# Attention 0: the softmax probabilities, split into fp16 halves, are transposed by DMA instead of by TensorE

## The chip, the cores and the metric

The kernel runs on one core of one Trainium2 chip. The metric is the device time of one execution in microseconds (us); lower is better. A core has TensorE (PE in the profile, with its weight loads as PEld), VectorE (DVE), ScalarE (ACT), GpSimd (POOL) and SyncE (SP), and 16 DMA engines that all queues share. An engine works through its own instructions in the order of the program and waits on semaphores.

## What is computed

A two-layer decoder over 32 sequences of 64 tokens of width 512. The change touches only the first attention, which has 32 query heads and 8 key/value heads of width 128:

```python
def _L0_xattn_ref(query, value, wq, wk, wv, wo):
    q = (query @ wq).reshape(b, tq, HQ, D)
    k = (key @ wk).reshape(b, tk, HKV, D)      # key = value = ctx_4096
    v = (value @ wv).reshape(b, tk, HKV, D)
    ...
    scores = jnp.einsum('bqhd,bkhd->bhqk', q, k)
    probs = jax.nn.softmax(scores, axis=-1)
    out = jnp.einsum('bhqk,bkhd->bqhd', probs, v).reshape(b, tq, HQ * D)
    return out @ wo

x = x + _L0_xattn_ref(_layernorm(x, axis=-1), ctx_4096, L0_xattn_wq, ...)
x = x + _L0_ffn_ref(_layernorm(x, axis=-1), L0_ffn_W0, ...)
x = x + _L1_xattn_ref(_layernorm(x, axis=-1), ctx_4096, ctx_4096, ...)
x = x + _L1_ffn_ref(_layernorm(x, axis=-1), L1_ffn_weight, ...)
```

Matrix products with fp32 accuracy are made from fp16 halves: a value is kept as high and low fp16 part, and a product takes three passes, high with high, high with low, low with high (`PASSES`).

## The kernel before

`attention0` walks over 8 groups (one key/value head and its 4 query heads) and in each over 4 blocks of 512 tokens (`t`, 8 sequences of 64). One block of one group is called a stage here; there are 32. Groups 0 to 6 run in a hardware loop (`Fori`), group 7 is written out. The stage is software-pipelined by hand: while the softmax of stage t runs on DVE and ACT, PE projects the queries, keys and values of the next stage. The order on PE in a stage, which no scheduler changes, is:

- `scores` (L534, into `sc`), for two pairs of heads, `jp` 0 and 1;
- `project` of the next stage, units 0 to 3: one query head each (L520, into the two banks `pj`; unit u waits until the low half of unit u-2 has left the same bank);
- `transpose_probs` (L543): eight 128x128 fp32 transposes of the probabilities `E` into the banks `tv`;
- in two stages of a group `transpose_weights` (L583), which prepares weights of the FFN that follows;
- `project` unit 4 (the keys, L520), `weigh_values` for the first half (L561, into `tv`), `project` unit 5 (the values, L525), `weigh_values` for the second half, and `project_out` (L572, into `xp`), which has 48 matmuls of 512 columns.

On DVE and ACT the scores lose their maximum (L743, L745), pass through the exponential (ACT, L666), and are summed, inverted and scaled (L751, L753, L755: `normalise`, which raises `p_done`). `E` holds [128 query rows of two heads, jp, 8 sequences, 64 keys] in fp32. After the transposes ACT copies `tv` to the high half of `PT` (L681) and DVE takes the low half (L788); `weigh_values` waits for `tp_lo`. Every projected unit leaves `pj` the same way: high half by ACT (L649, L651, L653), low half by DVE (L709, L712). `OT` is the weighted sum (L658, L718), `X` the residual that DVE adds to (L805). Once a group, at t = 0, the output weights are split: ACT L674, DVE L780.

SyncE's queue issues all DMAs: the weights of the next group (`load_qkv`, `load_o`), the FFN weights (L474, L476), and the stores of the prepared FFN weights (L481, L483).

Of the kernel before, what the change touches and what calls it, by code (L numbers as in the profile page):

```python
# [15 lines left out]
F16 = mybir.dt.float16  # L16
# [3 lines left out]
ALU = mybir.AluOpType  # L20
ACT = mybir.ActivationFunctionType
# [402 lines left out]
def attention0(nc, sb, pb, sem, X, ident, XT, CT, w0, w1, w0t_dram, w1t_dram, ahead_of_ffn0,  # L424
# [5 lines left out]
    with ExitStack() as ph:  # L430
# [7 lines left out]
        V = sb(ph, "V", [P, 2, 2, BT, HEAD0], F16)  # L438
        E = sb(ph, "E", [P, 2, BB, SEQ], F32)
        ST = sb(ph, "ST", [P, 3, 2, BB], F32)  # L440
        PT = sb(ph, "PT", [P, 2, BT, REP * SEQ], F16)
        OT = sb(ph, "OT", [P, 2, REP, BLOCK], F16)

        words = bits16(XB)
# [9 lines left out]
        names = ("o_hi o_lo sc_done pj_done tp_done pv_done xp_done "  # L454
                 "exp_done pj_hi tp_hi ot_hi max_done sub_done sum_done rcp_done p_done pj_lo tp_lo ot_lo x_acc "
                 "wb_ld wb2_ld wa_done wstep ww_done wcut wbits wm_done wsum wqs_done wq_done wt_done wt_hi wt_lo w_st")
        S = {n: sem(ph, "a0_" + n) for n in names.split()} | weight_sems
        block = ph.enter_context(nc.Block())
# [4 lines left out]
        def prepared(t, last):  # L463

            return [] if last else [(n, lo, hi) for n, (at, lo, hi) in enumerate(PREP) if at == t]

        def n_of(g, t, per, c):

            return g * (SPG * per) + (t * per + c)

        @block.sync
        def _(sp):
            with sp.Fori(0, GROUPS - 1) as g:
                sp.dma_start(WB[:, 0:8, :].rearrange("p (t c) k -> p t (c k)", t=2),  # L474
                             w0[bass.ds(g * 256, 256), :].rearrange("(t p) k -> p t k", p=P)).then_inc(S["wb_ld"], 16)
                sp.dma_start(WB[:, 8:16, :].rearrange("p (t c) k -> p t (c k)", t=4),  # L476
                             w1[:, bass.ds(g * 256, 256)].rearrange("(t p) k -> p t k", p=P)).then_inc(S["wb2_ld"], 16)
                sp.wait_ge(S["qkv_lo"], g * 2 + 2)
                load_qkv(sp, g + 1)
                sp.wait_ge(S["wt_lo"], g * 4 + 4)  # L480
                sp.dma_start(w0t_dram.rearrange("p (s c n) -> p s c n", s=2, c=KC)[:, :, :, bass.ds(g * 256, 256)],  # L481
                             WS0[:, :, :, :]).then_inc(S["w_st"], 16)
                sp.dma_start(w1t_dram.rearrange("p (s c n) -> p s c n", s=2, c=IC)[:, :, bass.ds(g * 2, 2), :],  # L483
                             WS1[:, :, :, :]).then_inc(S["w_st"], 16)

                sp.wait_ge(S["w_st"], g * 32 + 32)
                sp.wait_ge(S["o_lo"], g + 1)
                load_o(sp, g + 1)

            sp.wait_ge(S["qkv_lo"], 2 * GROUPS)  # L490
            sp.wait_ge(S["o_lo"], GROUPS)
            sp.dma_start(W0T[:, :, :, :], w0t_dram.rearrange("p (s c n) -> p s c n", s=2, c=KC)).then_inc(w0_ld, 16)

        @block.gpsimd
        def _(pool):
# [10 lines left out]
        def _(pe):  # L506
# [28 lines left out]
                                             KT[:, ka, b, :], start=n == 0, stop=n == 2)  # L535
                    last.then_inc(S["sc_done"], 1)

            def transpose_probs(g, t):
                pe.wait_ge(S["p_done"], n_of(g, t, 2, 2))
                for i in range(BT):  # L540
                    for jp in range(2):
                        at = (i % 2) * 256 + jp * P
                        last = pe.transpose(tv[i // 2][:, at:at + P],  # L543
                                            E[:, jp, 2 * i:2 * i + 2, :], ident[:, :])
                    if i % 2:
                        last.then_inc(S["tp_done"], 1)

            def weigh_values(g, t, pair):

                if pair == 0:
                    pe.wait_ge(S["pj_lo"], n_of(g, t, 6, 6))
                    pe.wait_ge(S["tp_lo"], n_of(g, t, 2, 2))
                else:
                    pe.wait_ge(S["ot_lo"], n_of(g, t, 4, 2))
                for s in range(2):
                    for n, (a, b) in enumerate(PASSES):
                        for h in range(2):
                            rows = slice(h * SEQ, (h + 1) * SEQ)  # L560
# [25 lines left out]
            def group(g, last):  # L586
                for t in range(SPG):
                    nxt = (g, t + 1) if t < SPG - 1 else (g + 1, 0)
                    more = not (last and t == SPG - 1)
                    scores(g, t)  # L590
                    if more:
                        project(*nxt, range(4))
                    transpose_probs(g, t)
# [39 lines left out]
        def _(act):  # L633
# [26 lines left out]
            def group(g, last):  # L660
                for t in range(SPG):
                    nxt = (g, t + 1) if t < SPG - 1 else (g + 1, 0)
                    more = not (last and t == SPG - 1)
                    for jp in range(2):
                        act.wait_ge(S["sub_done"], n_of(g, t, 2, jp + 1))
                        act.activation(E[:, jp, :, :], E[:, jp, :, :], ACT.Exp, scale=exp_scale).then_inc(S["exp_done"], 1)  # L666
                        if more:
                            high(*nxt, (jp,))
                    for p in prepared(t, last):
                        weights_times_rec(g, *p)  # L670
                    if t == 0:
# [3 lines left out]
                    if more:  # L675
                        high(*nxt, range(2, 4))
# [15 lines left out]
                    high_out(g, t, 1)  # L692
                    if t == SPG - 2 and not last:
                        high_kv(act, g + 1)
                    if last and t == SPG - 1:
                        first_x[0](act)

            high(0, 0, range(6))
            with act.Fori(0, GROUPS - 1) as g:
                group(g, False)  # L700
# [3 lines left out]
        def _(dve):  # L704
# [43 lines left out]
            def normalise(g, t, jp):  # L748
# [6 lines left out]
                dve.tensor_tensor(E[:, jp, :, :], E[:, jp, :, :], ST[:, 2, jp, :].unsqueeze(2).to_broadcast([P, BB, SEQ]),  # L755
                                  ALU.mult).then_inc(S["p_done"], 1)

            def group(g, last):
                for t in range(SPG):
                    nxt = (g, t + 1) if t < SPG - 1 else (g + 1, 0)  # L760
# [6 lines left out]

                    scores_less_max(g, t, 0)
                    scores_less_max(g, t, 1)
                    if more:  # L770
                        low(*nxt, 0)
                    normalise(g, t, 0)
                    if more:
                        low(*nxt, 1)
                    normalise(g, t, 1)
                    if more:
                        low(*nxt, 2)
                    if t == 0:
# [3 lines left out]
                    x_ahead(0)  # L782
                    if more:
                        low(*nxt, 3)
                    x_ahead(1)
# [1101 lines left out]
```

## Time and profile before

| | before |
|---|---|
| median of 3 runs | 1853.54 us (1852.3 to 3521.8) |
| profiled execution | 1853.57 us |
| its span | 1851.8 us |
| PE busy / DVE busy / ACT busy | 90% / 71% / 42% of the span |
| attention 0 (first to last of its stages) | about 60 to 1069 us of the span |

The span is the time from the first to the last instruction of the profile; the execution's time has 1.8 us around it. A row of a timeline has the start, the time that the engine was busy with this group of instructions, the engine, the line of the kernel and the operation as output<-input; a bracket at its end says how long the engine sat idle before it and what released it.

### The profile page before, as it was taken

How to read it: one execution, taken by the hardware profiler on the slowest of the kernel's cores; microseconds unless marked ns; L12 is line 12 of the kernel's file. 1: busy time of each engine (PE TensorE's matmuls, PEld its weight loads, DVE VectorE, ACT ScalarE, POOL GpSimd, SP SyncE). 2: the span in 40 equal slices, each digit the busy share in tenths (PEclk: the TensorE clock that was granted, in tenths of full speed). 3: DMA queues.
4: the chain of work that ended last, by engine and by line, in shares of the span. 5: the costliest groups of instructions: out<-in, count | busy, mean ns of one | idle time of the engine just before them, and what ended most of it. 6: DMA issues, size and time to landing. Idle time of an engine off the chain costs nothing. (4 is left out here: it accounts for less than half of the span.)

```text
span 1851.8 us, 31064 instructions
## 1 busy us (share of the span) xinstructions
PE 1666.5 (90%) x11590; PEld 936.3 (51%) x11590; DVE 1312.0 (71%) x2451; ACT 780.0 (42%) x1692; POOL 326.0 (18%) x266
## 2 busy tenths in 40 slices
PE   4899999999999999999999778999998696888793
PEld 4455555555555555555555434555554354555451
DVE  6567666776675666656757669887887535999688
ACT  3324242333243333423332245666665323555451
POOL 2001000010010000000100011111110224777414
PEclk8899999999999999999999889999999898999897
DMA  6100202002002020020030020000002001000002
GB/s 238 46 1 22 71 1 92 1 1 92 1 1 92 1 80 13 1 92 1 1 126 1 1 80 1 1 1 0 0 0 58 0 1 35 1 0 0 0 1 91
DMA packets 41663, 57.69 MB, mean 31 GB/s; under 512 B 1618, under 2 KB 23379, under 8 KB 41300
## 3 DMA queue, kind: packets, MB, share of 16 engines
q1 hardware_dynamic: 41556, 56.11, 8.9%
q8 instruction: 86, 1.41, 0.3%
q14 instruction: 21, 0.17, 0.0%
HBM read 44.57 MB, written 11.53 MB: 30 GB/s over the span
## 5 line engine op out<-in xcount | busy, mean ns | idle before, releaser
L520 PE MATMUL pj<-XT,WQ 128*128 128x512 f16 x1536 | 342.7, 384 | 6.4 <-PEq L330 6.4
L572 PE MATMUL xp<-WO,OT 128*128 128x512 f16 x1536 | 338.6, 380 | 1.8 <-DVE X L805 1.8
L520 PEld LDWEIGHTS pj<-XT,WQ 128*128 128x128 f16 x1536 | 149.6, 99 | 184.9 <-issue 7.9
L572 PEld LDWEIGHTS xp<-WO,OT 128*128 128x128 f16 x1536 | 147.7, 98 | 183.9 <-issue 11.8
L666 ACT ACTIVATE E<-E 128x512 f32<-128x512 f32 x64 | 40.2, 628 | 377.8 <-DVE E L745 377.8
L500 POOL TENSOR_TENSOR VW<-VW,XB 128x1024 f32<-128x1024 f32 x14 | 33.0, 2354 | 812.6 <-DVE VW L107 812.6
L805 DVE SCALAR_TENSOR_TENSOR X<-xp,X 128x512 f32<-128x512 f32 x128 | 88.2, 690 | 119.0 <-PE xp L572 118.0
L912 PE MATMUL db<-W0T,XD 128*128 128x448 f16 x768 | 160.0, 359 | 0.0
L709 DVE SCALAR_TENSOR_TENSOR QT<-pj,QT 128x512 f16<-128x512 f32 x128 | 88.4, 691 | 95.1 <-ACT QT L649 93.1
L938 PE MATMUL eb<-W1T,DT 128*128 128x512 f16 x672 | 150.9, 384 | 2.6 <-DVE DT L1088 2.6
L649 ACT ACTIVATE QT<-pj 128x512 f16<-128x512 f32 x128 | 76.1, 595 | 160.7 <-PE pj L520 160.7
L912 PEld LDWEIGHTS db<-W0T,XD 128*128 128x128 f16 x768 | 76.6, 100 | 71.1 <-issue 5.7
L938 PEld LDWEIGHTS eb<-W1T,DT 128*128 128x128 f16 x672 | 66.3, 99 | 84.3 <-DVE DT L1088 4.1
L525 PE MATMUL pj<-WKV,CT 128*128 128x128 f16 x1536 | 91.3, 219 | 0.0
L525 PEld LDWEIGHTS pj<-WKV,CT 128*128 128x128 f16 x1536 | 85.9, 98 | 6.8 <-issue 6.5
L988 ACT ACTIVATE VD<-DB,drec 128x128 f32<-128x128 bf16 x224 | 67.2, 387 | 51.7 <-DVE drec L85 51.7
L718 DVE TENSOR_TENSOR OT<-tv,OT 128x512 f16<-128x512 f32 x128 | 82.4, 685 | 9.0 <-ACT OT L658 4.5
L520 PE MATMUL pj<-CT,WKV 128*128 128x512 f16 x384 | 88.1, 379 | 0.0
L658 ACT ACTIVATE OT<-tv 128x512 f16<-128x512 f32 x128 | 69.5, 595 | 17.8 <-PE tv L561 17.8
L1376 POOL TENSOR_TENSOR E<-E,ST 128x512 f32<-128x512 f32 x64 | 65.3, 1042 | 55.3 <-DVE ST L1562 54.9
L998 ACT ACTIVATE VD<-VD,dscale 128x128 f32<-128x128 f32 x224 | 67.1, 388 | 18.7 <-DVE VD L1077 18.7
L1419 PE MATMUL a_tp<-ident,E 128*128 128x128 f32 x256 | 37.3, 293 | 38.9 <-POOL E L1376 38.9
(227 smaller groups left out, 2785.9 us busy)
## 6 DMA issues: line engine op xcount, KB each, us to landing
W0T<-in_L_xattn_wq SPq DMA_DIRECT2D x8, 1024.0 KB, 7.4
W0T<-in_L_xattn_wo SPq DMA_DIRECT2D x8, 1024.0 KB, 5.5
CS<-in_ctx SPq DMA_DIRECT2D x4, 1024.0 KB, 10.0
X<-in_x SPq DMA_DIRECT2D x4, 1024.0 KB, 11.2
out<-X SPq DMA_DIRECT2D x16, 256.0 KB, 2.0
XB<-in_L_ffn_W SPq DMA_DIRECT2D x14, 256.0 KB, 5.3
w0t<-XB SPq DMA_DIRECT2D x7, 512.0 KB, 3.6
w1t<-W0T SPq DMA_DIRECT2D x7, 512.0 KB, 4.1
```

Source lines behind the costliest of these rows:

```text
L520: last = pe.matmul(bank[:, :], w, src[:, b, k, tokens], start=n == 0, stop=n == 3 * KC - 1)
L525: last = pe.matmul(bank[:, i * P:(i + 1) * P], CT[:, a, k, own], WKV[:, b, k, 1, :], start=n == 0, stop=n == 3 * KC - 1)
L572: last = pe.matmul(xp[i % 2][:, :], OT[:, a, j, i * P:(i + 1) * P], WO[:, b, j, :], start=n == 0, stop=n == 3 * REP - 1)
L649: act.activation(QT[:, 0, :, u, :], q_bank(u), ACT.Copy, scale=UNSCALE).then_inc(S["pj_hi"], 1)
L658: act.activation(o_out(0, pair, h), o_bank(h), ACT.Copy).then_inc(S["ot_hi"], 1)
L709: dve.scalar_tensor_tensor(out=to[0], in0=q_bank(u), scalar=UNSCALE, in1=to[1], op0=ALU.mult, op1=ALU.subtract).then_inc(S["pj_lo"], 1)
L718: dve.tensor_tensor(o_out(1, pair, h), o_bank(h), o_out(0, pair, h), ALU.subtract).then_inc(S["ot_lo"], 1)
L805: dve.scalar_tensor_tensor(out=xt, in0=xp[i % 2][:, :], scalar=UNSCALE, in1=xt, op0=ALU.mult, op1=ALU.add).then_inc(S["x_acc"], 1)
L912: last = pe.matmul(db[q][:, 0:NQ], XD[:, i[1] % 2, a, k, :], W0T[:, b, k, q * NQ:(q + 1) * NQ], start=False, stop=n == 3 * KC - 1)
L938: last = pe.matmul(eb[:, :], DT[:, a, c, :], W1T[:, b, c, :], start=False, stop=c == IC - 1 and (a, b) == PASSES[-1])
L988: last = act.activation(VD[:, r, c, :], DB[:, r, c, :], ACT.Copy, scale=dr[:, r, c:c + 1])
L998: last = act.activation(VD[:, r, c, :], VD[:, r, c, :], ACT.Copy, scale=ds_[:, r, c:c + 1])
```

## The change

TensorE no longer transposes the probabilities. ACT writes the high fp16 half of the normalised `E` to a new SBUF buffer `EH` (L660 of the changed kernel), DVE the low half (L765), and SyncE issues, for each half, one DMA transpose [128 x 1024] fp16 from `EH` to `PT` (L478). `weigh_values` waits for both (`pt_done`, 32 per stage). `PT` has 128 key partitions as before, with another order of its columns. SyncE's queue in this phase holds these 64 transposes alone; the loads and stores that it issued are now issued by ACT, between its other work. DVE runs `normalise` of a head pair ahead of the low halves of the projected units, ACT both exponentials ahead of the first high half, and the split of the output weights has moved behind the fourth query unit.

```diff
-        PT = sb(ph, "PT", [P, 2, BT, REP * SEQ], F16)
+        EH = sb(ph, "EH", [P, 2, 2, BB * SEQ], F16)
+        PT = sb(ph, "PT", [P, 2, 2, BT, P], F16)
...
         @block.sync
         def _(sp):
-            with sp.Fori(0, GROUPS - 1) as g:
-                sp.dma_start(WB[:, 0:8, :].rearrange("p (t c) k -> p t (c k)", t=2),
...
-                sp.wait_ge(S["o_lo"], g + 1)
-                load_o(sp, g + 1)
...
+            for g in range(GROUPS):
+                for t in range(SPG):
+                    for part, split in enumerate(("e_hi", "e_lo")):
+                        sp.wait_ge(S[split], n_of(g, t, 2, 2))
+                        sp.dma_start_transpose(PT[:, part, :, :, :].rearrange("p j i n -> p (j i) n"),
+                                               EH[:, part, :, :].rearrange("p j n -> p (j n)")).then_inc(S["pt_done"], 16)
...
-            def transpose_probs(g, t):
-                pe.wait_ge(S["p_done"], n_of(g, t, 2, 2))
-                for i in range(BT):
-                    for jp in range(2):
-                        at = (i % 2) * 256 + jp * P
-                        last = pe.transpose(tv[i // 2][:, at:at + P],
-                                            E[:, jp, 2 * i:2 * i + 2, :], ident[:, :])
-                    if i % 2:
-                        last.then_inc(S["tp_done"], 1)
...
-                    pe.wait_ge(S["tp_lo"], n_of(g, t, 2, 2))
+                    pe.wait_ge(S["pt_done"], n_of(g, t, 32, 32))
...
-                                             PT[rows, b, 2 * pair + s, :], start=n == 0, stop=n == 2)
+                                             PT[rows, b, :, 2 * pair + s, :], start=n == 0, stop=n == 2)
...
+                    for jp in range(2):
                         if more:
                             high(*nxt, (jp,))
+                        act.wait_ge(S["p_done"], n_of(g, t, 2, jp + 1))
+                        act.activation(EH[:, 0, jp, :], E[:, jp, :, :].rearrange("p b k -> p (b k)"), ACT.Copy).then_inc(S["e_hi"], 1)
+                    if more:
+                        high(*nxt, range(2, 4))
...
-                    for i in range(2):
-                        act.wait_ge(S["tp_done"], n_of(g, t, 2, i + 1))
-                        act.activation(PT[:, 0, 2 * i:2 * i + 2, :], tv[i][:, :].rearrange("p (i n) -> p i n", i=2),
-                                       ACT.Copy).then_inc(S["tp_hi"], 1)
                     for p in prepared(t - 1, last):
+                        act.wait_ge(S["w_st"], g * 32 + 16)
                         high_weights(g, *p)
+                    if t == 0 and not last:
+                        load_weights(act, g)
...
+                    if t == 0 and not last:
+                        act.wait_ge(S["qkv_lo"], g * 2 + 2)
+                        load_qkv(act, g + 1)
+                    if t == 1 and not last:
+                        act.wait_ge(S["o_lo"], g + 1)
+                        load_o(act, g + 1)
+                    if t == SPG - 1 and not last:
+                        store_weights(act, g)
...
+            def low_probs(g, t, jp):
+                dve.wait_ge(S["e_hi"], n_of(g, t, 2, jp + 1))
+                dve.tensor_tensor(EH[:, 1, jp, :], E[:, jp, :, :].rearrange("p b k -> p (b k)"), EH[:, 0, jp, :],
+                                  ALU.subtract).then_inc(S["e_lo"], 1)
...
+                    normalise(g, t, 0)
                     if more:
                         low(*nxt, 0)
-                    normalise(g, t, 0)
+                    normalise(g, t, 1)
+                    low_probs(g, t, 0)
                     if more:
                         low(*nxt, 1)
-                    normalise(g, t, 1)
+                    low_probs(g, t, 1)
                     if more:
                         low(*nxt, 2)
...
-                    for i in range(2):
-                        dve.wait_ge(S["tp_hi"], n_of(g, t, 2, i + 1))
-                        dve.tensor_tensor(PT[:, 1, 2 * i:2 * i + 2, :], tv[i][:, :].rearrange("p (i n) -> p i n", i=2),
-                                          PT[:, 0, 2 * i:2 * i + 2, :], ALU.subtract).then_inc(S["tp_lo"], 1)
```

TensorE in the loop's second stage, before: from the last query unit to the first weighing.

```order
L520 MATMUL pj<-XT,WQ 128x512 x12
L539 REGISTER_ALU
L543 MATMUL tv<-ident,E 128x128 x8
L514 REGISTER_ALU
L520 MATMUL pj<-CT,WKV 128x512 x12
L561 MATMUL tv<-PT,V 128x256 x12
```

The same place of the changed kernel (its L551 is the weighing, L544 holds the wait for `pt_done`):

```order
L520 MATMUL pj<-XT,WQ 128x512 x12
L514 REGISTER_ALU
L520 MATMUL pj<-CT,WKV 128x512 x12
L544 REGISTER_ALU
L551 MATMUL tv<-PT,V 128x256 x12
```

The eight transposes are gone from between the units, and nothing has taken their place.

VectorE in the same stage, before: from the maximum of the second head pair to the third query unit (L709 is `low`, L755 the end of `normalise`).

```order
L745 TENSOR_TENSOR E<-sc,ST 128x512
L706 REGISTER_ALU
L709 SCALAR_TENSOR_TENSOR QT<-pj,QT 128x8x64
L751 TENSOR_REDUCE ST<-E 128x8
L753 RECIPROCAL ST<-ST 128x8
L755 TENSOR_TENSOR E<-E,ST 128x512
L706 REGISTER_ALU
L709 SCALAR_TENSOR_TENSOR QT<-pj,QT 128x8x64
L751 TENSOR_REDUCE ST<-E 128x8
L753 RECIPROCAL ST<-ST 128x8
L755 TENSOR_TENSOR E<-E,ST 128x512
```

And of the changed kernel (L714 is `low`, L760 the end of `normalise`, L765 the low half of the probabilities):

```order
L750 TENSOR_TENSOR E<-sc,ST 128x512
L756 TENSOR_REDUCE ST<-E 128x8
L758 RECIPROCAL ST<-ST 128x8
L760 TENSOR_TENSOR E<-E,ST 128x512
L711 REGISTER_ALU
L714 SCALAR_TENSOR_TENSOR QT<-pj,QT 128x8x64
L756 TENSOR_REDUCE ST<-E 128x8
L758 RECIPROCAL ST<-ST 128x8
L760 TENSOR_TENSOR E<-E,ST 128x512
L765 TENSOR_TENSOR EH<-E,EH 128x512
L711 REGISTER_ALU
L714 SCALAR_TENSOR_TENSOR QT<-pj,QT 128x8x64
```

One `low` now stands ahead of the second `normalise` where two stood, and the two low halves of the probabilities come around the second.

ScalarE in the same stage, of the changed kernel (L655 is the exponential, L638 a high half of a query unit, L660 the high half of the probabilities):

```order
L655 ACTIVATE E<-E 128x512
L654 REGISTER_ALU
L655 ACTIVATE E<-E 128x512
L636 REGISTER_ALU
L638 ACTIVATE QT<-pj 128x8x64
L660 ACTIVATE EH<-E 128x512
L636 REGISTER_ALU
L638 ACTIVATE QT<-pj 128x8x64
L660 ACTIVATE EH<-E 128x512
```

Before, a high half of a query unit stood between the two exponentials, and there was no L660; the two copies from `tv` stood behind the fourth query unit.

## Rows read from the trace of the kernel before

**Rows 1.** Windows, attention 0: stretch, engines' busy us (instructions), PEclk, DMA share, GB/s.
```profile
60.00:1033.50 973.50, 956.61 (x7498) 530.14 (x7497) 653.29 (x1094) 340.90 (x615) 59.49 (x28) 0.99 0.10 34
```
**Rows 2.** Waits of PE, 60 to 1040 us: waiter <- releaser: total us, times, longest.
```profile
PE sc L534 <- issue: 13.5, 6, 2.4
PE tv L561 <- DVE PT L788: 2.5, 2, 1.2
PE xp L572 <- DVE X L805: 1.8, 2, 0.9
```
**Rows 3.** Timeline of one stage (group loop, t = 1), 604 to 635 us.
```profile
604.51 1.56 PE L534 MATMUL sc<-KT,QT 128*128 128x64 f16 x48
605.91 10.52 PE L520 MATMUL pj<-XT,WQ 128*128 128x512 f16 x48
...
608.08 0.69 DVE L745 TENSOR_TENSOR E<-sc,ST 128x512 f32<-128x512 f32 x1
...
613.47 0.69 DVE L755 TENSOR_TENSOR E<-E,ST 128x512 f32<-128x512 f32 x1
...
616.27 1.04 PE L543 MATMUL tv<-ident,E 128*128 128x128 f32 x8
...
617.14 2.75 PE L520 MATMUL pj<-CT,WKV 128*128 128x512 f16 x12
...
619.83 0.83 PE L561 MATMUL tv<-PT,V 64*128 64x256 f16 x12
...
620.59 2.85 PE L525 MATMUL pj<-WKV,CT 128*128 128x128 f16 x48
...
634.51 1.56 PE L534 MATMUL sc<-KT,QT 128*128 128x64 f16 x48
```
**Rows 4.** Groups of instructions, 60 to 1040 us: count | busy us, mean ns | idle before.
```profile
L755 DVE TENSOR_TENSOR E<-E,ST 128x512 f32<-128x512 f32 x62 | 42.9, 692 | 2.1
L751 DVE TENSOR_REDUCE ST<-E 128x8 f32<-128x512 f32 x62 | 41.9, 675 | 0.0
L788 DVE TENSOR_TENSOR PT<-tv,PT 128x512 f16<-128x512 f32 x62 | 39.6, 680 | 0.0
L666 ACT ACTIVATE E<-E 128x512 f32<-128x512 f32 x62 | 38.9, 628 | 365.8 <-DVE E L745 365.8
L681 ACT ACTIVATE PT<-tv 128x512 f16<-128x512 f32 x62 | 33.5, 598 | 0.0
L780 DVE SCALAR_TENSOR_TENSOR WO<-W0T,WO 128x2048 f16<-128x2048 f32 x8 | 18.2, 2281 | 0.0
L674 ACT ACTIVATE WO<-W0T 128x2048 f16<-128x2048 f32 x8 | 15.2, 1902 | 0.0
L753 DVE RECIPROCAL ST<-ST 128x8 f32<-128x8 f32 x62 | 12.6, 203 | 2.1
```
**Rows 5.** DMA issues of the page: bytes each, median us from issue to landing.
```profile
out<-X SPq DMA_DIRECT2D x16, 256.0 KB, 2.0
w0t<-XB SPq DMA_DIRECT2D x7, 512.0 KB, 3.6
```
**Rows 6.** DMA queues of the page: packets, MB, share of 16 engines' span.
```profile
q1 hardware_dynamic: 41556, 56.11, 8.9%
```
**Rows 7.** DMA queue, 680 to 686 us, the two stores of a group alone.
```profile
q1 hardware_dynamic: 1312, 1.05, 51.6%
```
**Rows 8.** Timeline of the last stage (group 7, t = 3), 1047 to 1058 us.
```profile
1047.08 0.69 DVE L755 TENSOR_TENSOR E<-E,ST 128x512 f32<-128x512 f32 x1
...
1047.83 1.97 PE L543 MATMUL tv<-ident,E 128*128 128x128 f32 x8 [5.25 <-DVE E L755]
...
1051.30 1.46 PE L561 MATMUL tv<-PT,V 64*128 64x256 f16 x12 [1.50 <-DVE PT L788]
```
**Rows 9.** Timeline of PE behind attention 0, 1072 to 1079 us.
```profile
1072.75 0.53 PE L910 MATMUL db<-B0S,ones 128*128 128x448 bf16 x1 [3.14 <-DVE XD L1081]
1073.08 3.76 PE L912 MATMUL db<-W0T,XD 128*128 128x448 f16 x12
1076.68 0.35 PE L910 MATMUL db<-B0S,ones 128*128 128x448 bf16 x1
1076.87 2.43 PE L912 MATMUL db<-W0T,XD 128*128 128x448 f16 x12
```
**Rows 10.** Windows (columns of rows 1) around two idle times of PE.
```profile
696.30:698.70 2.40, 0.12 (x1) 0.00 (x0) 0.69 (x1) 0.00 (x0) 0.00 (x0) 1.00 0.02 4
698.70:701.00 2.30, 2.27 (x52) 1.81 (x53) 1.33 (x3) 0.00 (x0) 0.00 (x0) 1.00 0.03 7
1072.50:1074.50 2.00, 1.75 (x5) 0.73 (x6) 1.90 (x5) 0.21 (x1) 0.00 (x0) 0.50 0.93 401
```
**Rows 11.** Timeline of SyncE's queue: two issues of a group.
```profile
806.08 1.29 SPq L483 DMA_DIRECT2D w1t<-W0T  x1
810.41 0.39 SPq L277 DMA_DIRECT2D W0T<-in_L_xattn_wo  x1
```

More of the change, by code:

```diff
@@ L453, in attention0 @@
         xp = [pb(ph, f"xp{i}") for i in range(2)]
-        names = ("o_hi o_lo sc_done pj_done tp_done pv_done xp_done "
-                 "exp_done pj_hi tp_hi ot_hi max_done sub_done sum_done rcp_done p_done pj_lo tp_lo ot_lo x_acc "
+        names = ("o_hi o_lo sc_done pj_done pt_done pv_done xp_done "
+                 "exp_done pj_hi e_hi ot_hi max_done sub_done sum_done rcp_done p_done pj_lo e_lo ot_lo x_acc "
                  "wb_ld wb2_ld wa_done wstep ww_done wcut wbits wm_done wsum wqs_done wq_done wt_done wt_hi wt_lo w_st")
@@ L472, in _ @@
         def _(sp):
-            with sp.Fori(0, GROUPS - 1) as g:
-                sp.dma_start(WB[:, 0:8, :].rearrange("p (t c) k -> p t (c k)", t=2),
[L475 to L486, printed above, removed]
-                sp.wait_ge(S["o_lo"], g + 1)
-                load_o(sp, g + 1)
@@ L490, in _ @@
-            sp.wait_ge(S["qkv_lo"], 2 * GROUPS)
-            sp.wait_ge(S["o_lo"], GROUPS)
-            sp.dma_start(W0T[:, :, :, :], w0t_dram.rearrange("p (s c n) -> p s c n", s=2, c=KC)).then_inc(w0_ld, 16)
+            for g in range(GROUPS):
[4 more added lines that the diff above has]
+                                               EH[:, part, :, :].rearrange("p j n -> p (j n)")).then_inc(S["pt_done"], 16)
@@ new lines, in load_weights, with store_weights @@
+        def load_weights(queue, g):
+            queue.dma_start(WB[:, 0:8, :].rearrange("p (t c) k -> p t (c k)", t=2),
+                            w0[bass.ds(g * 256, 256), :].rearrange("(t p) k -> p t k", p=P)).then_inc(S["wb_ld"], 16)
+            queue.dma_start(WB[:, 8:16, :].rearrange("p (t c) k -> p t (c k)", t=4),
+                            w1[:, bass.ds(g * 256, 256)].rearrange("(t p) k -> p t k", p=P)).then_inc(S["wb2_ld"], 16)
+        def store_weights(queue, g):
+            queue.wait_ge(S["wt_lo"], g * 4 + 4)
+            queue.dma_start(w0t_dram.rearrange("p (s c n) -> p s c n", s=2, c=KC)[:, :, :, bass.ds(g * 256, 256)],
+                            WS0[:, :, :, :]).then_inc(S["w_st"], 16)
+            queue.dma_start(w1t_dram.rearrange("p (s c n) -> p s c n", s=2, c=IC)[:, :, bass.ds(g * 2, 2), :],
+                            WS1[:, :, :, :]).then_inc(S["w_st"], 16)
@@ L592, in group @@
                         project(*nxt, range(4))
-                    transpose_probs(g, t)
                     split = prepared(t - 1, last)
@@ L674, in group @@
                         act.activation(WO[:, 0, :, :], SO[:, :, :], ACT.Copy, scale=WEIGHT_SCALE).then_inc(S["o_hi"], 1)
-                    if more:
-                        high(*nxt, range(2, 4))
                     if last and t in (1, 2):
                         stats_x(act, t - 1)
-                    for i in range(2):
-                        act.wait_ge(S["tp_done"], n_of(g, t, 2, i + 1))
-                        act.activation(PT[:, 0, 2 * i:2 * i + 2, :], tv[i][:, :].rearrange("p (i n) -> p i n", i=2),
-                                       ACT.Copy).then_inc(S["tp_hi"], 1)
                     for p in prepared(t - 1, last):
+                        act.wait_ge(S["w_st"], g * 32 + 16)
                         high_weights(g, *p)
+                    if t == 0 and not last:
+                        load_weights(act, g)
                     if t == SPG - 2 and not last:
@@ L694, in group @@
                         high_kv(act, g + 1)
+                    if t == 0 and not last:
[6 more added lines that the diff above has]
+                        store_weights(act, g)
+                    if t == 1 and last:
+                        act.wait_ge(S["w_st"], 32 * (GROUPS - 1) + 16)
+                        act.wait_ge(S["qkv_lo"], 2 * GROUPS)
+                        act.wait_ge(S["o_lo"], GROUPS)
+                        act.dma_start(W0T[:, :, :, :], w0t_dram.rearrange("p (s c n) -> p s c n", s=2, c=KC)).then_inc(w0_ld, 16)
                     if last and t == SPG - 1:
                         first_x[0](act)
+            act.sem_inc(S["w_st"], 16)
             high(0, 0, range(6))
@@ L769, in group @@
                     scores_less_max(g, t, 1)
+                    normalise(g, t, 0)
                     if more:
                         low(*nxt, 0)
-                    normalise(g, t, 0)
+                    normalise(g, t, 1)
+                    low_probs(g, t, 0)
                     if more:
                         low(*nxt, 1)
-                    normalise(g, t, 1)
+                    low_probs(g, t, 1)
                     if more:
                         low(*nxt, 2)
+                    x_ahead(0)
+                    if more:
+                        low(*nxt, 3)
+                    x_ahead(1)
                     if t == 0:
@@ L781, in group @@
                                                  op0=ALU.mult, op1=ALU.subtract).then_inc(S["o_lo"], 1)
[L782 to L785, printed above, removed]
-                    for i in range(2):
-                        dve.wait_ge(S["tp_hi"], n_of(g, t, 2, i + 1))
-                        dve.tensor_tensor(PT[:, 1, 2 * i:2 * i + 2, :], tv[i][:, :].rearrange("p (i n) -> p i n", i=2),
-                                          PT[:, 0, 2 * i:2 * i + 2, :], ALU.subtract).then_inc(S["tp_lo"], 1)
                     for p in prepared(t - 1, last):
```

## The prediction, made before the changed kernel was run

> **What bounds the kernel now.** I began with the windows of attention 0: PE is busy 956.6 of 973.5 us at a granted clock of 0.99, VectorE 653, ScalarE 341 [rows 1]. So TensorE bounds this phase, and only what PE executes or waits for counts. The waits say how little it waits: 13.5 us without a releaser at six starts of a group, and 2.5 and 1.8 us on DVE [rows 2]. The timeline of one stage shows the period: scores start at 604.51 and again at 634.51, 30.0 us, and the pieces between lie end to end [rows 3]. The whole softmax chain runs beside the projection of the next stage, 605.91 to 616.4. The DMA engines are busy a tenth of the time. What PE does not have after the change is therefore a gain, unless it now waits at the weighing.
>
> **The change part by part.** All offsets are for the stage of rows 3, from its scores at 604.51.
>
> Transposes on PE. The eight L543 show as 1.04 us, but matmuls overlap in that view; from start to start the block takes 617.14 - 616.27 = 0.87 us [rows 3]. It runs in 32 stages. In 31 of them it lies on the path: 31 x 0.87 = 27 us, 1.5% of the time. That is the most the change can give in the steady part, so a gain of over 2% is nearly out of reach.
>
> Splitting on ACT and DVE. Two copies of about 0.6 us on ACT (L681, 598 ns) become two of the same size from SBUF, and two subtractions of 0.68 us on DVE (L788) become two of about 0.69, by L755, which also reads fp32 from SBUF [rows 4]. Both engines have idle time: ACT waits 365.8 us before its exponentials alone [rows 4]. I count nothing.
>
> When the halves are ready. Before, the second `normalise` ends at 613.47 + 0.69 = 614.16, with two `low` in front. Now the first sum follows the last subtraction of the maximum (608.08 + 0.69 = 608.77): sum 0.68, reciprocal and scaling 0.9 (L751, L753, L755 [rows 4]) to 610.4; one `low` to 611.0; sum, reciprocal and scaling to 612.6. ACT copies the second high half to about 613.3 (+8.8). DVE does the first low half, one `low`, the second low half: 614.7 (+10.2). Only the third query unit's bank comes close: its `low` ends near 613.9 when the fourth unit wants the bank at 605.91 + 3 x 2.63 = 613.8, a tenth of a us, counted at nothing.
>
> When they are wanted. Without L543 the key unit starts at 616.3 and the weighing comes 2.69 us later (619.83 - 617.14), at 619.0 (+14.5) [rows 3]. So the first DMA transpose has 5.7 us from its issue and the second 4.3 us. Behind that wait stand, on PE, both weighings, the value unit, `project_out` and the next scores: a late landing delays all of it by its own length, and the next stage cannot make it good.
>
> The DMA transposes. The trace of before has none. Each moves 256 KB inside SBUF, both on one queue. Below: a plain store of 256 KB from SBUF takes 2.0 us from issue to landing [rows 5]. Then both land in time and the stall is 0. Next up, by pieces: 128 partitions of 1024 elements, transposed in blocks of 128, give 1024 pieces of 256 B, 64 for each of 16 engines. The stores of a group occupied an engine for 0.516 x 6.0 x 16 / 1312 = 37.8 ns per packet [rows 7], giving 2.4 us a transpose. The mean over all packets of this execution is 0.089 x 1851.8 x 16 / 41556 = 63.5 ns [rows 6], giving 4.1 us. Above: both sides of a transpose can't be long runs. If an engine gathers 16 partitions, the destination gets runs of 32 B, 8192 pieces, at 37.8 ns / 16 each 19.4 us. Between ends of 2.0 and 19.4 I take 4.1, the piece price of the whole profile: a transposed piece should be dearer than the plain store's. The fixed part of a DMA I read as 2.0 us less 8 packets per engine at 63.5 ns, 1.5 us [rows 5, 6]. The two run one behind the other, so the last lands 2 x 4.1 + 1.5 = 9.7 us after the first issue, and PE waits 9.7 - 5.7 = 4.0 us in every stage.
>
> The Trainium skill speaks on both sides. "Advanced Engine Details and Errata", section X-Bar Transpose, says that trn2's transposing DMAs are as fast as regular ones; by that the sum would be that of the first rival. "VectorE: DVE Perf Modes", section The three transpose paths, gives 1309 ns for one 128x128 block by DMA against 390 ns on TensorE; as an estimate from that page eight blocks take 10.5 us, and that speaks against the change. No row here decides between them.
>
> The clock. After a stall of 2.3 us at a group's start the granted clock stays at 1.00 (2.4 GHz) [rows 10]. Behind 3.14 us of idle it is 0.50 (1.2 GHz) for the next work [rows 9, 10]: 0.53 for 0.35 and 3.76 for 2.43 us, 1.5 us lost until it is back [rows 9]. A stall of 4.0 us is on the far side, so I add 1.5 us a stage.
>
> The last stage has no projection to cover its softmax. From `p_done` (1047.8) to the weighing (1051.3) it took 3.5 us [rows 8]. Now: 0.6 for the high half and 9.7 for the transposes, 10.3: +6.8 us.
>
> Loads and stores on ACT. Eight issues a group, 0.39 to 1.29 us each [rows 11], 4 to 6 us of ACT, most at the end of a stage where ACT has nothing until the next exponential [rows 4]. Nothing, while that gap lasts. Their transfers end before the next transposes, 8.8 us into the stage. SyncE has nothing else in its queue to be held up. Moving the split of the output weights behind the fourth query unit (ACT 1.90, DVE 2.28 us [rows 4]) makes the first `OT` of stage 0 late: about 623.3 against a weighing that wants it at 622.5, 0.9 us in 8 stages, but only if PE does not stall before it.
>
> Sum: 1853.6 + 31 x (4.0 - 0.87 + 1.5) + 6.8 = 1853.6 + 143.5 + 6.8 = 2004 us. The profiled execution, 1853.57, equals the median of the runs, so nothing is shifted.
>
> **The rivals.** 1. The transposes are hidden, or almost. For it: 2.0 us for the same bytes, DMA engines idle nine tenths of the time, and 4.3 us of slack for the second. Against it: a transpose cannot be as few packets as that store. At 2.0 us: -27, +7 for the late `OT`, nothing in the last stage, 1834 us. At 2.4 us each: landing after 6.3, stall 0.6 and no fall of the clock, 31 x (0.6 - 0.87) = -8, last stage +3.4, 1849 us. This is the other side: it decides where both together take less than 5.7 + 0.87 = 6.6 us, 2.5 us each.
>
> 2. The transposes are served in short runs. For it: the 32-byte argument above. Against it: 19.4 us is a plain packet's price for a 32-byte one. At the bound: landing after 40.3, stall 34.6, 31 x (34.6 - 0.87 + 1.5) = 1092, last stage +37, 2983 us; at half that price about 2370. The skill's block price (above) as an estimate gives about 2410.
>
> 3. Faster by over 2%: below 1816.5. It would need more than PE's transposes, for instance the starts of groups [rows 2]; nothing in the diff touches them.
>
> **How the numbers follow.** Likeliest case (transposes of 3 to 7 us, PE stalls in every stage), 0.45, own range 1895 to 2250. Hidden or within 2%, 0.40. Short runs, above 2250, 0.12. Faster by over 2%, 0.03. About 2% is what a measurement of this kernel can tell from no change. Slower: 0.45 + 0.12 = 0.57; same 0.40; faster 0.03. The range 1828 to 2250 takes in rival 1 and leaves out rival 2 and 3.
>
> **What would show it.** In the changed profile the waits of PE should have the weighing (L551) waiting for the DMA into PT, 31 times about 4 us; the DMA issues should give issue to landing of PT<-EH, over 5 us; the windows of attention 0 should show a granted clock well below 0.99 and a period of 34 to 35 us. If the period is 29.1 to 29.4 with no such wait, rival 1 holds. If the wait is there but the clock stays at 1.00, the 1.5 us were wrong: 1957. If the wait is on DVE or ACT (EH late), my offsets are wrong. The forecast fails most simply if the transfer takes under 2.5 us or over 7.

## The result, and the profile after

| | before | after |
|---|---|---|
| median | 1854.07 us | 1837.57 us (1835.96 to 1841.43) |
| span of the profiled execution | 1851.8 us | 1838.9 us |
| start of the next phase (first transpose of the FFN on PE) | 1068.99 us | 1054.73 us |

The ratio is 0.992, with an interval of 0.9907 to 0.9932: 0.8% faster. One of the four runs of the kernel before took 3521.8 us; it counts in the median above and not in the ratio. The ratio lies inside 2%, on the side of the first rival and not of the forecast of 2004 us. All of the gain lies in attention 0; from the first transpose of the FFN to the end the two take 783 and 784 us.

The waits of PE in attention 0 of the changed kernel (waiter <- releaser: total us, times, longest) answer to [rows 2]:

```profile
PE tv L551 <- DVE OT L723: 15.9, 18, 2.0
PE pj L520 <- DVE QT L714: 12.5, 14, 0.9
PE tv L551 <- DMA PT<-EH: 10.8, 1, 10.8
PE xp L562 <- DVE X L813: 1.8, 2, 0.9
```

PE waits for the DMA once, in the last stage, and not 31 times. The 13.5 us without a releaser at the starts of groups are gone. In their place stand two waits that were not there: for `OT` before the second weighing, and for the low half of a query unit.

The window of attention 0 (columns as in [rows 1]) shows 20 us less of PE and twice the DMA share. Some 8 us of the 20 are the wait of the last stage, which falls into this window only after the change; from 60 to 1020 us PE is busy 944.3 us before and 932.7 after:

```profile
60.00:1033.50 973.50, 937.05 (x7326) 501.12 (x7324) 669.69 (x1125) 348.69 (x619) 59.54 (x28) 1.00 0.20 52
```

The transposes themselves: their instructions on SyncE's queue (ns: min/median/max) and, at the end of the same answer, their time from issue to landing.

```profile
L478 SPq DMA_TRANSPOSE PT<-EH x64: 1232/1305/2317, 81.8 to 1032.8; - x64
...
DMA to landing us min/median/max: 2.8/2.9/4.6
```

The DMA engines from 602 to 607 us, in which two transposes and nothing else are in flight:

```profile
q1 hardware_dynamic: 2112, 0.52, 46.5%
```

So the count of the prediction was nearly right, 1056 pieces of 256 B for each where it had 1024; the price was not: 0.465 x 5.0 x 16 / 2112 = 17.6 ns a piece, 1.2 us a transpose. The same stage on the timeline (a group's second, scores at 593.45), to be read against [rows 3]:

```profile
600.74 0.69 DVE L760 TENSOR_TENSOR E<-E,ST 128x512 f32<-128x512 f32 x1
...
601.46 0.63 ACT L660 ACTIVATE EH<-E 128x512 f16<-128x512 f32 x1 [0.64 <-DVE E L760]
...
602.12 2.58 SPq L478 DMA_TRANSPOSE PT<-EH  x2
602.55 0.68 DVE L765 TENSOR_TENSOR EH<-E,EH 128x512 f16<-128x512 f32 x1
...
605.29 2.75 PE L520 MATMUL pj<-CT,WKV 128*128 128x512 f16 x12
...
607.98 0.83 PE L551 MATMUL tv<-PT,V 64*128 64x256 f16 x12
```

The first transpose is issued 8.7 us after the scores, the second right behind it; the last lands at 602.12 + 1.3 + 2.9 = 606.3, 1.7 us before PE comes to the weighing. In the first stages of the seven looped groups a transpose takes longer, 3.7 to 4.6 us from issue to landing. In each of these seven stages the engines carry a 16 KB packet of the queue "instruction" meanwhile, as in the one from 571.83 on (the engines' rows, and the time to landing):

```profile
q1 hardware_dynamic: 2048, 0.52, 78.2%
q8 instruction: 1, 0.02, 1.4%
...
DMA to landing us min/median/max: 3.7/4.0/4.3
```

There, from 571.8 to 576.2 us, a piece takes 0.782 x 4.4 x 16 / 2048 = 26.9 ns, and the last lands 1.4 us before the weighing. The other 50 transposes take 2.8 to 3.1 us. That the packet is what slows the 14 is not tested.

### The profile page after: what moved, and what is told of

Same layout as the page of the kernel before. It is cut to its first block and busy times, and to the rows that moved or that the text cites. A ratio compares the mean times of both kernels' runs of the same rounds, so it can differ in the third digit from the quotient of the medians.

```text
span 1838.9 us, 30560 instructions
## 1 busy us (share of the span) xinstructions
PE 1642.4 (89%) x11334; PEld 903.3 (49%) x11334; DVE 1316.7 (72%) x2451; ACT 785.6 (43%) x1692; POOL 326.4 (18%) x266
## 5 line engine op out<-in xcount | busy, mean ns | idle before, releaser
L520 PE MATMUL pj<-XT,WQ 128*128 128x512 f16 x1536 | 343.5, 380 | 18.9 <-DVE QT L714 12.5
L520 PEld LDWEIGHTS pj<-XT,WQ 128*128 128x128 f16 x1536 | 145.5, 98 | 202.3 <-DVE QT L714 31.0
L562 PEld LDWEIGHTS xp<-WO,OT 128*128 128x128 f16 x1536 | 148.1, 98 | 184.6 <-issue 13.2
L655 ACT ACTIVATE E<-E 128x512 f32<-128x512 f32 x64 | 40.4, 632 | 380.2 <-DVE E L750 380.2
L714 DVE SCALAR_TENSOR_TENSOR QT<-pj,QT 128x512 f16<-128x512 f32 x128 | 87.9, 687 | 80.2 <-ACT QT L638 78.4
L638 ACT ACTIVATE QT<-pj 128x512 f16<-128x512 f32 x128 | 75.7, 591 | 115.4 <-PE pj L520 115.4
L551 PE MATMUL tv<-PT,V 64*128 64x256 f16 x768 | 54.3, 275 | 26.6 <-DVE OT L723 15.9
```

The source lines that it names most:

```text
L520: last = pe.matmul(bank[:, :], w, src[:, b, k, tokens], start=n == 0, stop=n == 3 * KC - 1)
L562: last = pe.matmul(xp[i % 2][:, :], OT[:, a, j, i * P:(i + 1) * P], WO[:, b, j, :], start=n == 0, stop=n == 3 * REP - 1)
L638: act.activation(QT[:, 0, :, u, :], q_bank(u), ACT.Copy, scale=UNSCALE).then_inc(S["pj_hi"], 1)
L714: dve.scalar_tensor_tensor(out=to[0], in0=q_bank(u), scalar=UNSCALE, in1=to[1], op0=ALU.mult, op1=ALU.subtract).then_inc(S["pj_lo"], 1)
```

## Experiments

Periods below are the distances of the starts of a stage's scores on the timeline, for the four stages of a group. "Length" is the time from the first scores to the first transpose of the FFN: 994.3 us before (74.69 to 1068.99), 981.5 in the changed kernel (73.22 to 1054.73). The kernel before has 30.0, 30.0, 30.9 and 30.9 us and, at six starts of groups, 2.1 to 2.4 us of idle; behind three of these the first stage takes 31.6 us. The changed kernel has 29.7, 29.2, 32.5 and 31.2 us. Each ratio is taken against runs of the kernel before on the same chip; two runs of the changed kernel itself have lengths of 981.5 and 980.3 us.

### Is the cost of a transpose hidden, and by how much? Twice the transposes

```diff
+                        for x in range(1 if g < GROUPS - 1 else 0):
+                            sp.dma_start_transpose((PX0, PX1)[part][:, x, :, :], EH[:, part, :, :]...).then_inc(S["pt_done"], 16)
                         sp.dma_start_transpose(PT[:, part, :, :, :]...
```

> The changed kernel with each DMA transpose issued twice in groups 0 to 6 (28 stages): an extra one of the same source into an unused buffer ahead of each, and the weighing waits for all four. It doubles the disputed cost. From the changed kernel's trace one transpose occupies the DMA engines for 1.7 us and 1.2 us are fixed, so the last lands 4 x 1.7 + 1.2 = 8.0 us after the first issue, against 6.4 us that PE leaves: a stall of 1.6 us in 28 stages without a fall of the clock, about +45 us on 1838, 1883. The pricing of my prediction (4.1 us a transpose) would have it at 4 x 4.1 + 1.5 - 5.7 = 12.2 us of stall a stage, over 2200 us.

Measured: 1879.57 us, ratio 1.0152 (1.0132 to 1.0173). PE waits for the DMA 42.2 us in 17 places (10.2 of them in the last stage), and the length is 1023.0 us, 41.5 more than in the changed kernel. The pricing of the prediction, 12.2 us of stall a stage, is refuted by a wide margin. My own estimate of +45 us was near by luck: it had 1.6 us in each of 28 stages, from the 1.7 us of a disturbed stage, while the extra time lies in the first stages (3.1 to 3.8 us of wait, 33 of the 41.5 us), is 1.0 us in the second, 0 in the third and under 0.9 in the fourth.

### Three times the transposes

> The changed kernel with each DMA transpose issued three times in 28 stages, two extra ones into unused buffers ahead of each. It makes the stall that my prediction assumed: the last lands 6 x 1.7 + 1.2 = 11.4 us after the first issue, 5.0 us after PE wants it. If the rest of my reasoning holds (a stall is paid in full in every stage, and behind more than 3 us of idle the granted clock is at half for a while, 1.5 us each), this is 28 x (5.0 + 1.5) = +182 us on 1838, about 2020. If the clock does not fall: 1978, granted clock about 1.00 in attention 0.

Measured: 1965.43 us, ratio 1.0616 (1.0593 to 1.0639). Waits of PE, and the timeline of PE in two stages of this kernel:

```profile
PE tv L559 <- DMA PT<-EH: 111.9, 29, 10.2
```

```profile
129.73 1.45 PE L559 MATMUL tv<-PT,V 64*128 64x256 f16 x12 [3.67 <-DMA PT<-EH]
131.12 3.83 PE L529 MATMUL pj<-WKV,CT 128*128 128x128 f16 x48
...
165.43 0.83 PE L559 MATMUL tv<-PT,V 64*128 64x256 f16 x12 [2.79 <-DMA PT<-EH]
166.19 2.85 PE L529 MATMUL pj<-WKV,CT 128*128 128x128 f16 x48
```

And the windows behind these two waits and one ahead of the second (columns as in [rows 1]):

```profile
129.70:133.00 3.30, 3.27 (x30) 2.60 (x31) 1.15 (x2) 1.08 (x2) 0.00 (x0) 0.51 0.02 5
...
162.00:165.40 3.40, 0.64 (x3) 0.10 (x1) 1.29 (x2) 3.38 (x5) 0.00 (x0) 1.00 0.72 160
165.40:168.90 3.50, 3.47 (x60) 3.18 (x60) 1.98 (x3) 1.08 (x2) 0.00 (x0) 1.00 0.02 5
```

Behind a wait of 3.67 us the granted clock is 0.51 (1.2 GHz), and the weighing and the value unit take 5.28 instead of 3.68 us: 1.6 us lost, where the prediction had 1.5. Behind the 2.79 us shown it stays at 1.00. So the prediction's size of this loss holds. The length of the wait alone does not decide whether it comes. Of the 13 stages here that wait 2.8 us three are followed by the lower clock, and in the kernel with twice the transposes 3.33 us are not and 3.07 us are (last two pairs; granted clock 1.00 and 0.58 over the 3.5 us behind them):

```profile
867.75 1.46 PE L559 MATMUL tv<-PT,V 64*128 64x256 f16 x12 [2.80 <-DMA PT<-EH]
869.14 5.10 PE L529 MATMUL pj<-WKV,CT 128*128 128x128 f16 x48
...
221.38 0.83 PE L559 MATMUL tv<-PT,V 64*128 64x256 f16 x12 [3.33 <-DMA PT<-EH]
222.14 2.85 PE L529 MATMUL pj<-WKV,CT 128*128 128x128 f16 x48
...
735.66 1.46 PE L559 MATMUL tv<-PT,V 64*128 64x256 f16 x12 [3.07 <-DMA PT<-EH]
737.06 3.60 PE L529 MATMUL pj<-WKV,CT 128*128 128x128 f16 x48
```

All 15 waits of 3.5 us and more in the looped stages of the kernel with three transposes are followed by the lower clock. The time is 1965 and not 2020 us because the stall was shorter than I expected: SyncE issues a transpose every 1.31 us, and this sets their distance, since the engines need only 1.2 us of it: 6 x 1.31 + 1.6 = 9.5 us. From 222.37 the timeline shows 1.6 us for the issue of a transpose while ACT's loads are being issued, and the stall there is 4.81 us.

### Where did the idle time at the starts of groups go? Loads on ACT alone

Edit: the kernel before, with `load_weights`, `store_weights`, `load_qkv` and `load_o` on ACT as in the change; the rest untouched.

> The kernel before with one part of the change: the loads and stores of this phase are issued by ACT at the places of the changed kernel, SyncE issues none; the probabilities are still transposed by PE. Theory G (group starts): the 2.3 us that PE stood idle at each start of a group, 13.5 us in all, came from the bulk loads of the SyncE queue that were in flight when the loop jumped back, and not from anything in the transposes. It expects the group starts without that idle time, stages otherwise as before (30.0, 30.0, 30.9, 30.9 us) and about 1840 us. Rival: the group starts were shortened by the transposing part, or the idle time is the jump itself; then 1854 us and 13.5 us idle again.

Measured: 1832.36 us, ratio 0.9895 (0.9878 to 0.9912), faster than the whole change. The length is 975.9 us, the periods are 30.0, 30.0, 30.9 and 30.9 us, and no wait at a group's start is left among PE's waits. The 18.4 us by which it is shorter than before are more than the 13.5 us of idle. The other 4.9 us are the three first stages of 31.6 us, which take 30.0 here. Windows of the kernel before, behind the idle at 446.96 and behind the one at 698.73:

```profile
449.00:451.00 2.00, 2.00 (x8) 0.67 (x6) 1.57 (x3) 0.63 (x1) 0.00 (x0) 0.50 0.00 0
700.50:702.50 2.00, 2.00 (x11) 0.88 (x9) 1.84 (x3) 0.63 (x1) 0.00 (x0) 1.00 0.00 0
```

Both idle times are 2.3 us. Behind three of the six the granted clock falls to 0.50 (1.2 GHz), behind three it stays at 1.00.

### Queue or moment? SyncE's loads wait for the group's first scores

```diff
             with sp.Fori(0, GROUPS - 1) as g:
+                sp.wait_ge(S["sc_done"], g * 8 + 1)
                 sp.dma_start(WB[:, 0:8, :].rearrange("p (t c) k -> p t (c k)", t=2),
```

> The kernel before with one wait more: SyncE issues the first load of a group only after the first scores of that group are done (about 2 us after the group has begun), all still on SyncE's queue. Theory G expects the same as from the loads on ACT: no idle time of about 2.3 us at a group's start, about 1840 us. If it is the queue (SyncE or ACT) and not the moment that counts, it stays at 1854 us.

Measured: 1832.60 us, ratio 0.9898 (0.9882 to 0.9915), the same as with the loads on ACT. So it is the moment. Before, a group's first FFN weights were issued 12 us ahead of its first scores (686.67 against 698.73); here they are issued 1.1 us behind them. In the kernel before, PE waits for nothing that the profile shows, after the jump back of the loop:

```profile
698.73 0.46 PE L534 MATMUL sc<-KT,QT 128*128 128x64 f16 x10 [2.31 <-issue]
```

Until 695.8 us the DMA engines are full of the loads issued from 685.8 on, and a packet of the queue "instruction" comes through behind them, at 696.25 us; PE is idle from 696.42. Rows of the kernel before from 696 to 697 us, then of this experiment from 680 to 681 us, at the same place of its loop (packet at 680.65, scores at 683.39, no idle time ahead of them):

```profile
q1 hardware_dynamic: 66, 0.03, 10.7%
q8 instruction: 1, 0.02, 5.9%
```

```profile
q8 instruction: 1, 0.02, 7.1%
```

In the experiment that packet has the engines to itself and comes while PE still works. In both kernels the scores start 2.5 to 2.9 us behind it at all six jumps. Ahead of group 7, where the loop ends and no FFN weights are loaded, the kernel before has no idle time either. That the loop's instructions queue behind bulk loads fits these rows and both experiments; which engine's instructions the packet carried the rows don't say, so the mechanism is argued, the moment of the loads is shown.

### The order of the query units

```diff
-                    normalise(g, t, 0)
                     if more:
                         low(*nxt, 0)
-                    normalise(g, t, 1)
-                    low_probs(g, t, 0)
+                    normalise(g, t, 0)
                     if more:
                         low(*nxt, 1)
+                    normalise(g, t, 1)
+                    low_probs(g, t, 0)
                     low_probs(g, t, 1)
```

and on ACT the high half of each query unit right behind its exponential, as before.

> The changed kernel with the order of before on DVE and ACT for the query units and the normalisation (low, normalise, low, normalise; a high half between the exponentials), both low halves of the probabilities behind it. Theory D: the reordering, made so that EH is ready earlier, costs 12.5 us of PE waiting for the low half of a query unit in the two stages of a group with FFN weights, where the scaling of E runs into GpSimd's multiplication and takes 1.45 instead of 0.69 us; with the old order these waits go, the scaling takes 0.69 us in all 64, and the DMA still lands about when PE wants it (e_lo at +11.6, landing 2.9 us later at +14.5, wanted at +14.5). About -12 us, 1826. Rival: the new order is needed, the transposes now land late and PE waits for them in most stages, 0.5 us or more each; then no gain or a loss of up to 16 us, with the wait at the weighing on the DMA.

Measured: 1829.66 us, ratio 0.9863 (0.9847 to 0.9879); the length is 969.8 us, 11.7 less than in the changed kernel. The scaling takes 0.69 us in all 64, and the waits for query units are gone:

```profile
PE tv L551 <- DMA PT<-EH: 18.4, 8, 10.7
PE tv L551 <- DVE OT L723: 13.7, 11, 2.0
```

The periods are 30.3, 29.2, 31.2 and 30.1 us. In seven stages, the first ones of the groups, the DMA is now 1.1 us late. Theory D holds in its size, 11.7 us of length for 12 (the time is 1829.66 for 1826); the edit moves the order on DVE, the order on ACT and the collision with GpSimd together, so it does not say which of them PE waited for.

### OT in time

Edit, on ACT: scaling of FFN weights and split of the output weights between the third and the fourth query unit, `high_q` behind both halves of `OT`; on DVE the low half of the output weights ahead of the fourth query unit.

> The changed kernel with ACT's and DVE's work around the weighing put where the sum is not late: the scaling of FFN weights and the split of the output weights between the third and the fourth query unit, the high half of the next group's query weights behind both halves of OT. Theory O: the 15.9 us that PE waits before the second weighing (18 times) are ACT's queue, 1.2 us in each third stage and 0.5 in each first; they go, the waits for the query units stay, and the time falls by 12 to 16 us to about 1824. Rival: the wait only moves to the next stage's query units or to the key unit, under 4 us gained.

Measured: 1829.91 us, ratio 0.9876 (0.986 to 0.9893). The waits for `OT` fall from 15.9 to 3.8 us, while those for `X` grow from 1.8 us (2 times) to 6.1 (9 times); the length is 972.7 us, 8.8 less. That is more than the rival's 4 and less than my 12 to 16.

### Both

> Both edits at once (the order of before for the query units; ACT's work around the weighing moved). If the two losses are independent, as theories D and O have it, the gains add: about 1838 - 25 = 1813 us, and stages of 29.1 and 30.0 us. If one hides the other, the time is near the better of the two alone.

Measured: 1827.16 us, ratio 0.9856 (0.984 to 0.9873). My 1813 us were missed. The length is 968.3 us, 13.2 less than in the changed kernel, and not 20.5 as the sum of the two: the first stage takes 30.6 us, 1.4 of it in a wait for the DMA.

### The loads out of the transposes' way

```diff
                         act.activation(E[:, jp, :, :], E[:, jp, :, :], ACT.Exp, scale=exp_scale).then_inc(S["exp_done"], 1)
+                        if jp and t == 0 and not last:
+                            load_weights(act, g)
```

> e7 (both edits) with the loads of FFN weights in the first stage of a group issued right behind the two exponentials, 4 to 5 us into the stage, instead of 12 us into it, where they are in flight with the transposes of that stage. In e7 the first stage takes 30.6 us, with 1.4 us of PE waiting for the DMA into PT, the second stage 29.2. Theory L: that wait is the collision of the transposes with the 512 KB of loads; then the first stage falls to about 29.2, 7 x 1.4 = 10 us, 1817 us. Rival: the transposes are late in the first stage by themselves (EH is not ready earlier there); the wait stays and the time is that of e7.

Measured: 1821.11 us, ratio 0.9827 (0.9805 to 0.9848), the fastest of all kernels here. The waits of PE:

```profile
PE tv L551 <- DMA PT<-EH: 10.9, 2, 10.8
PE xp L562 <- DVE X L814: 6.1, 9, 0.9
PE tv L551 <- DVE OT L724: 5.2, 3, 2.0
```

The first stage falls from 30.6 to 29.5 us in six of seven groups, and the length from 968.3 to 961.9 us, two thirds of the 10 us that I expected. The longest time of a transpose from issue to landing falls from 4.3 to 3.1 us. Theory L holds: the loads that share the DMA engines with the transposes made them late.

### The collision with GpSimd

```diff
                     pool.wait_ge(S["wq_done"], g * 2 + (n + 1))
+                    pool.wait_ge(S["p_done"], n_of(g, t + 1, 2, 1))
                     pool.tensor_tensor(v, v, ws[:, lo:hi].unsqueeze(2).to_broadcast([P, hi - lo, P]), ALU.mult)...
```

> The changed kernel with one wait more on GpSimd: its multiplication of FFN weights starts only when the first scaling of E in the stage is done. Theory C (contention): the scaling takes 1.45 instead of 0.69 us in the 14 stages in which it meets that multiplication, and this is what makes the low half of the first query unit late and PE wait 0.9 us there. Then all first scalings take 0.69 us, the 12.5 us of PE waiting for DVE's low halves fall to under 4, and the time by about 10 us to 1828. Rival: the length of the scaling has another cause, or PE's wait comes from the order alone (a whole normalisation ahead of the low half); then the wait stays near 12 us and the time at 1838.

> The changed kernel again, beside the two above on the same chip. Both theories: as before, ratio near 0.992, about 1838 us, 12.5 us of waits for the query units and 15.9 us for OT.

Measured on one chip: the changed kernel again 1837.12 us, ratio 0.9918 (0.9898 to 0.9938), with waits of 12.5 and 15.8 us; with the wait on GpSimd 1835.53 us, ratio 0.9909 (0.9889 to 0.993). The two ratios can't be told apart; the trace can. In the changed kernel, third stage of a group:

```profile
627.19 1.90 POOL L502 TENSOR_TENSOR VW<-VW,wscale 128x1024 f32<-128x1024 f32 x1
...
628.19 1.45 DVE L760 TENSOR_TENSOR E<-E,ST 128x512 f32<-128x512 f32 x1
629.56 0.68 DVE L714 SCALAR_TENSOR_TENSOR QT<-pj,QT 128x512 f16<-128x512 f32 x1
...
630.30 5.52 PE L520 MATMUL pj<-XT,WQ 128*128 128x512 f16 x24 [0.90 <-DVE QT L714]
```

With the wait on GpSimd, the same stage:

```profile
626.28 0.69 DVE L761 TENSOR_TENSOR E<-E,ST 128x512 f32<-128x512 f32 x1
...
627.05 1.90 POOL L503 TENSOR_TENSOR VW<-VW,wscale 128x1024 f32<-128x1024 f32 x1 [1.85 <-DVE E L761]
...
628.44 1.05 DVE L761 TENSOR_TENSOR E<-E,ST 128x512 f32<-128x512 f32 x1
```

The scaling on DVE ends 0.55 us behind GpSimd's multiplication, nearly as if it had begun when that ended (alone it takes 0.69). Moved away, the first scaling takes 0.69 us, and the second meets the multiplication instead (1.05). PE's waits for DVE's low halves fall from 12.5 to 5.0 us, the length from 980.3 to 975.6 us. Theory C holds for the larger part of the wait, though I had expected under 4 us of it to be left; the gain of 10 us that I expected was too high, since the collision only moved. The Trainium skill says so in "SBUF — State Buffer", section Who interferes with whom: a DVE instruction with two SBUF inputs and a GpSimd instruction that reads SBUF exclude one another. The trace agrees, with 1.45 for 0.69 us; the instructions of DVE that read `pj` from PSUM took 0.69 us beside the same multiplication before the change.

## Why the prediction was wrong, point by point

**What bounds the kernel**: right. PE's removed work, 27 us by the prediction, is in the result, a little smaller: the second stage of a group falls by 0.79 us, from 30.0 to 29.2, against 0.87 predicted. The missing 0.08 is the "tenth of a us" at the query unit's bank.

**When the halves are ready and wanted**: right. The first transpose was issued at +8.7 in that stage against +8.8, and PE came to the weighing at +14.5 as predicted.

**The DMA transposes**: the step that failed. "Between ends of 2.0 and 19.4 I take 4.1, the piece price of the whole profile." The count nearly held; an undisturbed piece cost 17.6 ns instead of 63.5, below even the 37.8 ns of [rows 7], whose packets are three times as large. A transpose thus took 1.2 us of the engines instead of 4.1. From the first issue to the last landing it took 4.2 us instead of 9.7: 1.3 us of issue to the second, and 2.9 us from its issue to landing. The stall is 0. My lower bound, 2.0 us by the store in [rows 5], was the nearer one, and the argument that a transposed piece must be dearer had no row behind it. I had a mean price over packets of all sizes; a price per byte (0.516 x 6.0 / 4 = 0.8 us by [rows 7]), or the time of the store of the same 256 KB, would each have put the stall at 0.

The 32-byte runs of rival 2 don't show either: 0.52 MB in 2112 packets are 256 B each.

**The clock**: the size was right (1.5 predicted, 1.6 measured behind 3.67 us in the kernel with three transposes), but there was no stall for it to follow. The sentence that after 2.3 us of idle at a group's start "the granted clock stays at 1.00" was read from one of six starts; behind three of the other five it falls, in the same trace.

**The last stage**: +6.8 predicted. From its scores (1023.67) to the weighing (1036.00) it is 12.3 us, before 10.3 [rows 8 show its later part]; with a `project_out` of 12.80 us for 11.76 it is about +3. The transposes took 4.9 us there from the first issue to the weighing, not 9.7.

**Splitting, "I count nothing"; the query unit's bank, "a tenth of a us, counted at nothing"**: wrong in two of four stages. There the last FFN work delays DVE, the scaling runs into GpSimd (0.76 us), and PE waits 0.9 us for a query unit: 12.5 us in all. With the order of before these stages are 1.2 us shorter each, so that about 17 us hang on the order. My times came from a stage without that work.

**Loads and stores on ACT, "Nothing"**: wrong twice. The late `OT` was foreseen at 0.9 us in 8 stages; it was 0.47 us in the first stages, and 1.2 us in each third stage, where ACT's scaling, `high_weights` and `high_q` had come to stand in front of it. And the loads moved away from the starts of groups, which gave 18 us of attention 0 by itself, 13.5 of idle and 4.9 at the lower clock: with the loads on ACT alone its length is 975.9 us, before 994.3. I had said of the starts of groups that "nothing in the diff touches them"; the issue time of the loads did.

So the sum is another than each of my cases. Loads moved: about -18. PE's transposes: 31 x 0.79, -24.5. The two waits for `PT` of [rows 2]: -2.5. Last stage: +3. Query units: +17. `OT`: +14 (15.9 less the 2.0 that was there in the last stage). That gives -11; the length fell by 12.8, and the rest I can't assign. The transposing part alone costs 5.6 us against loads on ACT alone (975.9 to 981.5). The first rival had the right mechanism for the transposes and came within 4 us, but partly since a gain and losses that it did not know cancelled.

## To carry to other kernels

When a bulk transfer is in flight as a hardware loop jumps back, look for idle time without a releaser behind the jump: one wait on SyncE, which moved the loads 13 us, was worth 1% here, more than the change itself. An operation taken from the bound engine pays only if the order on the others stays in time: read it in the busiest stage of the cycle, not in a typical one. And price a transfer that the trace doesn't show by the row with the same bytes, not by the mean of all packets. Read what follows an idle time at all its places: one row of six said that 2.3 us cost no clock.

## What the hardware showed that I had not expected

- A DMA transpose of 128x1024 fp16 from SBUF to SBUF lands 2.9 us after its issue (2.8 at best, 3.7 to 4.6 in the first stages of the groups) and takes 1.31 us of SyncE's queue, 1.2 us of the DMA engines; several in a row follow at the distance of the issue.
- Idle time of 2.3 us on PE at a loop's jump, gone when the loads start 1.1 us behind the group's first scores instead of 12 us ahead of them.
- The clock can fall to 1.2 GHz behind 2.3 us of idle and stay at 2.4 GHz behind 3.3 us; equal idle times of 2.8 us had both outcomes.
- A DVE operation with two SBUF inputs took 1.45 instead of 0.69 us beside GpSimd's multiplication.
